# Splitting the experts' weights into fp16 halves on the chip, in place of fp32 matmuls

## The chip, the cores and the metric

The kernel runs on one core of a Trainium2 chip, in one launch. The metric is the device time of an execution in microseconds. Five engines work side by side, each through its own queue in order: TensorE (PE, whose weight loads are shown apart as PEld), VectorE (DVE), ScalarE (ACT), GpSimd (POOL), and SyncE (SP), which only issues the transfers here. They wait for one another through counting semaphores.

## The reference

Two layers of a perceiver: cross-attention to a context of 4096 rows, a self-attention, and a feed-forward part, for 2 batches of 256 latents of width 256, all in fp32. The change concerns the last block, a small attention followed by a mixture of 8 experts:

```python
xf = x.reshape(S, D)                                   # S = 512 rows, D = 256
gates = softmax(xf @ wg); idx = argmax(gates)
loc = ...                                              # place of the row among those of its expert
keep = loc < cap                                       # cap = 64 rows for each expert
disp = zeros((E * cap, D)).at[slot].set(xf, mode='drop').reshape(E, cap, D)
h = einsum('ecd,edf->ecf', disp, w1) + b1[:, None, :]  # D = 256 -> FF = 1024, no activation
y = (einsum('ecf,efd->ecd', h, w2) + b2[:, None, :]).reshape(E * cap, D)
out = where(keep, gate_val * y[slot], 0)
```

Each expert's `w1` is 256 x 1024 and its `w2` 1024 x 256, one MB each, so the 16 matrices make 16 MB.

## The kernel before

Every engine's program is written out by hand, and the order of its instructions is fixed by the source. The low-rank attention (`low_rank_attention`, 16 heads, 2 batches) comes ahead of the last block. It is a software pipeline of 32 steps `i`: PE does scores (L758), turns the normalised probabilities (`turn5`, L770), mixes (`mix5`, L785) and projects (`out5`, L801); ACT takes the exponentials (L1193) and high halves (`hi5` L1200, `oT` L1206); DVE takes maxima (L1644), normalises (`norm5`: L1655, and two `tensor_scalar` of 128x256 at L1657) and makes low halves (`lo5` L1649, `oT_lo` L1705). Its matmuls are already made of fp16 halves: high times high, high times low, low times high. POOL makes the low halves of the heads' weights (`vo_lo`, L1340) in the first 16 steps. In the later steps, tables of step numbers (`LAST_AT`) let in the first pieces of the last block: layer norm, the qkv projection (PE L871, evicted by DVE L1678), and the products of queries and keys, done for one half of the latents by POOL (`queries_times_keys`, L364) and for the other by DVE.

`last_attention` follows. DVE adds the bias to qkv (L1792), multiplies queries with keys (L364), reduces (L1737), applies the softmax in small steps (L1740, L1741, L1746 to L1748), takes the values (L1754, L1756), and applies a layer norm (L1779, L1784). Each of these waits for the one before, and PE fills its time with matmuls whose result nobody reads (`keep_busy`, L470). POOL takes a power for each norm (L1360) and adds biases to rows (L1348, L1349).

`experts`: DVE works out each row's slot and writes a selection matrix `Sm` of zeros and ones (L1827); PE gathers the experts' rows with it (L928), transposed, from the rows' fp16 halves `y1` into PSUM, and ACT and DVE evict that into `disT` in fp32. The experts then go in 4 pairs `g`. `hidden(g)` (L951) multiplies with `w1` in fp32: the first expert of a pair uses the left 64 columns of the array and the second the right 64. ACT and DVE evict (L1261, L1846), `turn_hidden(g)` (L962) turns the result in 8 pieces, DVE adds the bias and evicts (L1853, two of 128x512), and `down(g)` (L976) multiplies with `w2` in fp32, again the pair side by side. `y_out` (DVE L1859, ACT L1237, DVE L1861) and `combine(g)` (L985) bring the rows back. PE's order is hidden 0, turn 0, hidden 1, down 0, turn 1, hidden 2, down 1, combine 0, turn 2, hidden 3, down 2, combine 1, turn 3, down 3, combine 2, combine 3. Two layer norms of DVE and the store end the kernel.

The experts' weights are loaded by SP early enough in whatever part of SBUF has come free: `w1` of experts 4 and 5 before the low-rank attention, 0 to 3 in its middle, `w2` near its end, and `w1` of 6 and 7 once `m_o` has been counted twice.

Of the kernel before, what the change touches and what calls it, by code (L numbers as in the profile page):

```python
# [179 lines left out]

FILL_BETWEEN = {0: 8, 3: 6, 11: 52, 12: 6, 13: 16, 20: 8}
# [24 lines left out]
def build(nc, x, ctx, consts, cols, w_x, w_a, w_ao, b_a, w_f1, w_f2, w_f3, w_f4, w_g1, w_g2, w_g3, w_y, w_yv, b_yv,  # L206
          w_l, w_vo, w_in, w_out, rows6, w_gate, w_e1, b_e1, w_e2, b_e2, consts6, out):
    with ExitStack() as stack:
# [124 lines left out]
        disT = tail[:, 2048:3072].rearrange("p (c n) -> p c n", c=DC)  # L333
        yy = tail[:, 3072:4096].bitcast(F16).rearrange("p (g h n) -> p g h n", g=E6 // 2, h=2)
        hh = [tail[:, 1024:2048], work[:, 3072:4096]]
        hT = [rest[:, 2048 + 1024 * i:3072 + 1024 * i].rearrange("p (f n) -> p f n", f=FC) for i in range(2)]
# [33 lines left out]
        def _(sp):  # L370
# [45 lines left out]
            load_w1 = lambda e: sp.dma_start(w1[:, e], w_e1[e].rearrange("(c p) f -> p c f", p=P)).then_inc(s("w1_in%d" % e), 16)  # L416
            load_w2 = lambda e: sp.dma_start(w2[e], w_e2[e].rearrange("(f p) d -> p f d", p=P)).then_inc(s("w2_in%d" % e), 16)
            def load_vo(q):

                if q >= 2:  # L420
                    sp.wait_ge(s("vo_hi"), 2 * q - 2)
                    sp.wait_ge(s("vo_lo"), 2 * q - 2)
                sp.dma_start(vo_stage[:, 2 * (q % 2):2 * (q % 2) + 2], w_vo[2 * q:2 * q + 2].rearrange("h (c p) n -> p h c n", p=P))\
                    .then_inc(s("x_in%d" % (q % 2)), 16)
# [9 lines left out]
            sp.wait_ge(s("vo_hi"), H5)  # L434
            sp.wait_ge(s("vo_lo"), H5)
# [29 lines left out]
        def _(pe):  # L465
# [259 lines left out]
            def low_rank_attention():  # L725
# [64 lines left out]
                def out5(i):  # L790
                    b = i // H5
                    pe.wait_ge(s("l_ot_lo"), i + 1)
                    pe.wait_ge(s("vo_lo"), min(i + 1, H5))
# [112 lines left out]
            def experts():  # L906
# [17 lines left out]
                for t in range(NT):  # L924
                    pe.wait_ge(s("m_S"), t + 1)
                    for c in range(DC):
                        for h in range(2):
                            mm = pe.matmul(ps[:, c, :], y1[:, h, t, c * P:(c + 1) * P], Sm[:, t, :], start=(t == 0 and h == 0),  # L928
                                           stop=(t == NT - 1 and h == 1))
                        if t == NT - 1:  # L930
                            mm.then_inc(s("m_dis_ps"), 1)
# [6 lines left out]
                def hidden(g):  # L938

                    if g == 0:  # L940
                        pe.wait_ge(s("m_dis"), 2)
# [23 lines left out]
                def down(g):  # L965
# [3 lines left out]
                    for e in pair:  # L969
                        pe.wait_ge(s("w2_in%d" % e), 16 * (1 + (e < SLOTS - 2) * DEEP // SLOTS))  # L970
                    for half in range(2):
                        pe.wait_ge(s("m_hT"), 2 * g + 1 + half)
                        for f in range(half * FC // 2, (half + 1) * FC // 2):
                            for e in pair:
                                o = 64 * (e % 2)
                                mm = pe.matmul(ps[o:o + 64, 4, 0:D], hT[g % 2][:, f, o:o + 64], w2[e][:, f, :],  # L976
                                               start=(f == 0), stop=(f == FC - 1), skip_group_check=True)
# [45 lines left out]
        def _(act):  # L1023
# [143 lines left out]

            def low_rank_attention():
                def vo_hi(h):
# [4 lines left out]
                    act.activation(vo[:, h, 0], vo_stage[:, h % 4], ACT.Copy).then_inc(s("vo_hi"), 1)  # L1174
# [36 lines left out]
                for i in range(2 * H5 + 4):  # L1211
# [22 lines left out]
            def last_part():  # L1234
# [4 lines left out]
                second = leave_pair(1, 7)  # L1239
                next(second)  # L1240
                for j in range(2):
# [3 lines left out]
                    if j == 0:  # L1245
                        next(second)
                    else:
# [4 lines left out]
                act.wait_ge(s("m_dis_ps"), 1)  # L1252
                act.activation(disT[:, 0, :], ps[:, 0, :], ACT.Copy).then_inc(s("m_dis"), 1)
# [3 lines left out]
                for g in range(E6 // 2):  # L1257
# [4 lines left out]
                    if g:  # L1262
                        y_hi(g - 1)
                y_hi(E6 // 2 - 1)
# [23 lines left out]
        def _(pool):  # L1288
# [48 lines left out]
            for h in range(H5):  # L1337

                pool.wait_ge(s("vo_hi"), h + 1)
# [628 lines left out]
```

## Time and profile before

| | us |
|---|---|
| median of 3 timed executions | 567.11 |
| lowest and highest of them | 566.3 and 569.16 |
| the profiled execution's own time | 566.04 |
| its span, first to last instruction | 564.2 |
| granted TensorE clock, mean over the span | 0.985 of full speed |

The span is what all rows of the trace lie in. The profiled execution takes 1.84 us beyond its span, and it is 1.1 us faster than the median of the timed ones. PE is the busiest engine (518.3 us, 92%), then DVE (353.8 us, 63%), ACT (283.5 us, 50%) and POOL (76.7 us, 14%). Part of PE's busy time is the filling matmuls.

### The profile page before, as it was taken

How to read it: one execution, taken by the hardware profiler on the slowest of the kernel's cores; microseconds unless marked ns; L12 is line 12 of the kernel's file. 1: busy time of each engine (PE TensorE's matmuls, PEld its weight loads, DVE VectorE, ACT ScalarE, POOL GpSimd, SP SyncE). 2: the span in 40 equal slices, each digit the busy share in tenths (PEclk: the TensorE clock that was granted, in tenths of full speed). 3: DMA queues.
4: the chain of work that ended last, by engine and by line, in shares of the span. 5: the costliest groups of instructions: out<-in, count | busy, mean ns of one | idle time of the engine just before them, and what ended most of it. 6: DMA issues, size and time to landing. Idle time of an engine off the chain costs nothing.

```text
span 564.2 us, 9402 instructions
## 1 busy us (share of the span) xinstructions
PE 518.3 (92%) x3556; PEld 357.1 (63%) x3556; DVE 353.8 (63%) x848; ACT 283.5 (50%) x616; POOL 76.7 (14%) x66
## 2 busy tenths in 40 slices
PE   7899998998999898999989988899999999888992
PEld 6565664565666554557555776788888778664551
DVE  4874646964449854275555655698878787744335
ACT  3777952537731038494267726788855444011110
POOL 0134131200012000000002400333201011200001
PEclk9999999999999999999999999899999999989997
DMA  8974680000000000000500040222183006950001
GB/s 273 321 198 85 113 187 0 1 2 1 1 1 0 5 25 0 2 1 0 208 17 1 2 150 1 76 75 78 61 316 133 1 1 191 352 204 1 1 0 38
DMA packets 45197, 44.06 MB, mean 78 GB/s; under 512 B 18656, under 2 KB 41184, under 8 KB 45024
## 3 DMA queue, kind: packets, MB, share of 16 engines
q1 hardware_dynamic: 45152, 43.45, 25.3%
q8 instruction: 29, 0.48, 0.4%
q14 instruction: 16, 0.13, 0.1%
HBM read 38.73 MB, written 0.52 MB: 70 GB/s over the span
## 4 chain that ended last, share of the span: by engine, by line
PE 66%; DVE 16%; issue 9%; ACT 6%; POOL 1%; DMA 1%; SPq 0%; DVEq 0%; ACTq 0%; POOLq 0%
PE ps L648 10%; PE ps L677 8%; PE ps L785 7%; PE ps L801 7%; PE ps L662 4%; PE ps L679 4%; PE ps L736 3%; PE ps L770 3%; PE ps L951 3%; PE ps L976 2%; PE ps L758 2%; PE ps L871 1%; DVE mx L1538 1%; ACT arena L1129 1%; ACT arena L1114 1%
## 5 line engine op out<-in xcount | busy, mean ns | idle before, releaser
L648 PE MATMUL ps<-ctx_tr,qtl 128*128 128x512 f16 x384 | 90.7, 379 | 2.1 <-ACT arena L1129 1.4
L1538 DVE TENSOR_REDUCE mx<-arena 128x1 f32<-128x512 f32 x64 | 43.1, 682 | 35.3 <-ACT arena L1129 34.7
L648 PEld LDWEIGHTS ps<-ctx_tr,qtl 128*128 128x128 f16 x384 | 36.7, 98 | 40.8 <-issue 3.2
L1129 ACT ACTIVATE arena<-ps 128x512 f32<-128x512 f32 x64 | 37.9, 596 | 43.9 <-PE ps L648 43.8
L677 PE MATMUL ps<-ctx_nat,pth 128*128 128x512 f16 x172 | 58.4, 379 | 0.0
L1114 ACT ACTIVATE arena<-arena,small 128x512 f32<-128x512 f32 x64 | 45.8, 716 | 6.3 <-DVE small L1547 6.2
L801 PE MATMUL ps<-arena,ctx_tr 128*128 128x256 f16 x384 | 47.2, 273 | 0.1
L679 PE MATMUL ps<-ctx_nat,ptl 128*128 128x256 f16 x172 | 46.9, 273 | 0.0
L662 PE MATMUL ps<-const,arena 128*128 128x128 f32 x256 | 39.1, 275 | 5.8 <-ACT arena L1114 5.1
L1293 POOL TENSOR_TENSOR rstd<-mv,col 128x2 f32<-128x2 f32 x13 | 10.0, 766 | 245.3 <-DVE mv L1398 245.2
L1552 DVE TENSOR_TENSOR ptl<-ps,pth 128x512 f16<-128x512 f32 x43 | 29.5, 688 | 21.6 <-ACT pth L1122 21.4
L662 PEld LDWEIGHTS ps<-const,arena 128*128 128x128 f32 x256 | 29.8, 140 | 17.8 <-ACT arena L1114 10.9
L801 PEld LDWEIGHTS ps<-arena,ctx_tr 128*128 128x128 f16 x384 | 37.5, 98 | 4.6 <-DVE ctx_tr L1705 0.3
L1200 ACT ACTIVATE pth<-ps 128x512 f16<-128x512 f32 x32 | 19.0, 594 | 33.7 <-PE ps L770 33.6
L470 PE MATMUL ps<-ones 128*128 128x256 f16 x244 | 31.7, 291 | 1.1 <-DVE ones L1883 1.1
L1193 ACT ACTIVATE ctx_tr<-ps,small 128x256 f32<-128x256 f32 x64 | 29.6, 471 | 5.7 <-DVE work L1644 5.6
L1122 ACT ACTIVATE pth<-ps 128x512 f16<-128x512 f32 x43 | 25.4, 591 | 9.0 <-PE ps L662 8.8
L470 PEld LDWEIGHTS ps<-ones 128*128 128x128 f16 x244 | 25.2, 104 | 6.2 <-DVE ones L1883 1.1
L677 PE MATMUL ps<-ctx_nat,arena 128*128 128x512 f16 x84 | 28.7, 379 | 0.0
L1644 DVE TENSOR_SCALAR_CACHE_REDUCE work<-ps 128x256 f16<-128x256 f32 x64 | 24.4, 418 | 6.4 <-PE ps L758 6.3
L1552 DVE TENSOR_TENSOR arena<-ps,arena 128x512 f16<-128x512 f32 x21 | 14.5, 690 | 21.0 <-ACT arena L1122 20.8
L677 PEld LDWEIGHTS ps<-ctx_nat,pth 128*128 128x128 f16 x172 | 16.8, 98 | 17.0 <-issue 1.4
(294 smaller groups left out, 1041.0 us busy)
## 6 DMA issues: line engine op xcount, KB each, us to landing
ctx_nat<-in_w_e SPq DMA_DIRECT2D x8, 1024.0 KB, 7.2
ctx_tr<-in_w_e SPq DMA_DIRECT2D x6, 1024.0 KB, 11.8
work<-in_ctx SPq DMA_DIRECT2D x8, 512.0 KB, 5.2
ctx_tr<-in_ctx SPq DMA_DIRECT2D x8, 512.0 KB, 7.4
work<-in_w_vo SPq DMA_DIRECT2D x8, 512.0 KB, 3.8
ctx_nat<-in_w_l SPq DMA_DIRECT2D x4, 512.0 KB, 5.2
arena<-in_w_e SPq DMA_DIRECT2D x2, 1024.0 KB, 7.2
wts<-in_rows SPq DMA_DIRECT2D x1, 1024.0 KB, 14.0
```

The lines of the kernel that those rows point to most:

```text
L470: pe.matmul(ps[:, to, 0:SEQ], o[:, 0:P], o, start=True, stop=True, skip_group_check=True)
L648: mm = pe.matmul(ps[:, n % 2, :], qtl[:, qh, d, u * P:(u + 1) * P], CT[:, t0:t0 + KT, kh, d, :], start=(i == 0 and d == 0), stop=(i == 2 a ...
L662: mm = pe.transpose(ps[:, 4 + j % 2, i * P:(i + 1) * P], S[:, (j) % SRING, i * P:(i + 1) * P], ident)
L677: pe.matmul(ps[:, acc, :], PH[j % PRING][:, i * P:(i + 1) * P], CN[:, t].rearrange("p h d -> p (h d)"), start=(c == 0 and i == 0), stop=Fa ...
L679: mm = pe.matmul(ps[:, acc, 0:D], PL[j % PRING][:, i * P:(i + 1) * P], CN[:, t, 0, :], start=False, stop=(c == NCH - 1 and i == KT - 1), s ...
L785: mm = pe.matmul(ps[:, 4 + i % 2, d * SEQ:(d + 1) * SEQ], xl5[b][:, xh, u, d * P:(d + 1) * P], pt[:, i % 2, pu], start=(n == 0), stop=(n = ...
L801: mm = pe.matmul(ps[:, 6 + b, t * D:(t + 1) * D], oT5[:, i % 2, oh, c, p * P:(p + 1) * P], vo[:, h, vh, c, :], start=(i % H5 == 0 and p == ...
L1114: act.activation(S[:, j % SRING, :], S[:, j % SRING, :], ACT.Exp, bias=ebias[:, u:u + 1], scale=SCALES[L], accum_out=ls[:, u, c:c + 1]).th ...
L1129: act.activation(S[:, n % SRING, :], ps[:, n % 2, :], ACT.Copy).then_inc(s("score_copied"), 1)
L1193: act.activation(P5[:, i % 2, t, :], ps[:, i % 2, t * SEQ:(t + 1) * SEQ], ACT.Exp, bias=nb5[:, i % 2, t:t + 1], scale=1.0 / 16, accum_out= ...
L1538: dve.tensor_reduce(mx[:, u, c:c + 1], S[:, n % SRING, :], AX.X, ALU.max).then_inc(s("score_max"), 1)
L1552: dve.tensor_tensor(PL[j % PRING], ps[:, 4 + j % 2, :], PH[j % PRING], ALU.subtract).then_inc(s("pt_lo"), 1)
```

## The change

The 28 halves of the matrices ("units" of 128x1024 fp32 numbers, half of one expert's `w1` or `w2`) of all experts but `w2` of experts 0 and 1 are split on the chip: ACT writes the fp16 high half (`unit_high`), and POOL subtracts it from the fp32 number and writes the fp16 low half (`unit_low`) over the first half of the unit's own place. The second half of that place becomes the home of a later unit's high half (`HOMES`), so that a later copy of ACT waits for an earlier subtraction of POOL. `disT` and the hidden rows `hT` are kept as fp16 halves too, and each fp32 product becomes three fp16 products.

```diff
+UNITS = [(1, e, k) for e in (4, 5, 0, 1, 2, 3) for k in range(2)] \
+    + [(2, e, k) for e in (6, 7, 2, 3) for k in range(2)] + [(1, e, k) for e in (6, 7) for k in range(2)] \
+    + [(2, e, k) for e in (4, 5) for k in range(2)]
+HOMES = ["a", "b", 0, 1, 2, 3, 4, 5, 6, 7, 8, 9, "c", "d", "e", 10, 11, 12, 13, 14, "f", "g", 15, 16, 17, 18, 19, 20]
+SPLIT_AT = (15, 16, 17, 18, 21, 22, 24, 25, 26, 28, 29, 30)
...
     # PE
-                            mm = pe.matmul(ps[:, c, :], y1[:, h, t, c * P:(c + 1) * P], Sm[:, t, :], start=(t == 0 and h == 0),
-                                           stop=(t == NT - 1 and h == 1))
+                            mm = pe.matmul(ps[:, 6 * h + c, :], y1[:, h, t, c * P:(c + 1) * P], Sm[:, t, :], start=(t == 0),
+                                           stop=(t == NT - 1))
...
                 def hidden(g):
...
-                    for e in pair:
-                        pe.wait_ge(s("w1_in%d" % e), 16)
+                    pe.wait_ge(s("w_lo"), H5 + units_until(1, g))
                     for f in range(2):
                         for c in range(DC):
-                            for e in pair:
-                                o = 64 * (e % 2)
-                                mm = pe.matmul(ps[o:o + 64, f, :], disT[:, c, e * CAP:(e + 1) * CAP],
-                                               w1[:, e, c, f * 512:(f + 1) * 512], start=(c == 0), stop=(c == DC - 1))
+                            for k, (th_, wh) in enumerate(((0, 0), (1, 0), (0, 1))):
+                                for e in pair:
+                                    o = 64 * (e % 2)
+                                    mm = pe.matmul(ps[o:o + 64, f, :], disT[:, th_, c, e * CAP:(e + 1) * CAP],
+                                                   unit_halves(1, e, c)[wh][:, f * 512:(f + 1) * 512],
+                                                   start=(c == 0 and k == 0), stop=(c == DC - 1 and k == 2), skip_group_check=True)
...
     # down(g): g == 0 keeps its fp32 form; for g >= 1 it waits for w_lo and does the same three products with w2
...
     # ACT
+            def unit_high(n):
...
+                act.activation(unit_hi(n), unit_place(n), ACT.Copy).then_inc(s("w_hi"), 1)
...
+                    for n in range(12):
+                        if SPLIT_AT[n] == i:
+                            unit_high(n)
...
+                for n in range(12, 16):
+                    unit_high(n)
...
+                        for f in range(2):
+                            act.wait_ge(s("m_hw"), 2 * g - 1 + f)
+                            act.activation(hT[g % 2][:, 0, 4 * f:4 * f + 4, :], hTw[:, 4 * f:4 * f + 4, :], ACT.Copy).then_inc(s("m_hT_hi"), 1)
...
     # POOL
+            def unit_low(n):
+                pool.wait_ge(s("w_hi"), H5 + n + 1)
+                pool.tensor_tensor(unit_lo(n), unit_place(n), unit_hi(n), ALU.subtract).then_inc(s("w_lo"), 1)
...
                 if k == 0:
                     biases(2, slice(3, 4))
+                    for n in range(12, 17):
+                        unit_low(n)
+                if k == 1:
+                    pool.wait_ge(s("m_S"), NT)
+                    for n in range(17, 28):
+                        unit_low(n)
...
     # DVE
-                    for t in range(2):
-                        o = dve.tensor_scalar(P5[:, i % 2, t, :], P5[:, i % 2, t, :], l5[:, i % 2, t:t + 1], 1024.0, ALU.mult, ALU.mult)
-                    o.then_inc(s("l_norm"), 1)
+                    both = l5[:, i % 2, :].unsqueeze(2).broadcast_to([P, 2, SEQ])
+                    dve.scalar_tensor_tensor(P5[:, i % 2], P5[:, i % 2], 1024.0, both, ALU.mult, ALU.mult).then_inc(s("l_norm"), 1)
...
-                dve.tensor_copy(disT[:, 1, :], ps[:, 1, :]).then_inc(s("m_dis"), 1)
+                for c in range(DC):
+                    dve.wait_ge(s("m_dis_ps"), 2 * c + 2)
+                    dve.tensor_copy(disT[:, 1, c, :], ps[:, 6 + c, :]).then_inc(s("m_dis"), 1)
...
+                    for f in range(2 if g else 0):
+                        dve.wait_ge(s("m_hT_hi"), 2 * g - 1 + f)
+                        dve.tensor_tensor(hT[g % 2][:, 1, 4 * f:4 * f + 4, :], hTw[:, 4 * f:4 * f + 4, :],
+                                          hT[g % 2][:, 0, 4 * f:4 * f + 4, :], ALU.subtract).then_inc(s("m_hT"), 1)
```

ACT's other units stand at these places: 16 to 19 after its second `oT6` eviction (L1230), 20 to 23 after the exponential of the gates (L1251), 24 to 27 after its first eviction of hidden rows. POOL's units 0 to 4 follow the heads' weights, 5 to 8 follow the biases of the first layer norm of the last block, and 9 to 11 those of the second, ahead of its product of queries and keys. The semaphores `vo_hi` and `vo_lo` are now called `w_hi` and `w_lo` and count on; the loads of SP keep their order and their places.

Order on POOL in the changed kernel, from the power of the last block's first residual norm (L1449) to the end of the kernel's splitting; the rows of 128x1024 at L1423 are `unit_low`:

```order
L1449 TENSOR_TENSOR work<-work,col 128x2 [waits m_var]
L1433 TENSOR_TENSOR ctx_tr<-ctx_tr,wts 128x256 [waits xn_turned,w6_in]
L1434 TENSOR_TENSOR X<-X,wts 128x256
L1423 TENSOR_TENSOR arena<-arena,pth 128x1024 [waits w_hi]
L1423 TENSOR_TENSOR arena<-arena,ptl 128x1024 [waits w_hi]
L1423 TENSOR_TENSOR arena<-arena,work 128x1024 [waits w_hi]
L1423 TENSOR_TENSOR arena<-arena,ctx_nat 128x1024 [waits w_hi]
L1423 TENSOR_TENSOR ctx_tr<-ctx_tr,ctx_nat 128x1024 [waits w_hi]
L1449 TENSOR_TENSOR work<-work,col 128x2 [waits m_var]
L1423 TENSOR_TENSOR ctx_tr<-ctx_tr,arena 128x1024 [waits w_hi,m_S]
```

Before, POOL's queue had nothing after the two bias additions (L1433 and L1434 above) but the remaining powers. Now five units stand between them and the next power, and eleven behind that one, of which the list shows the first.

Order on DVE in the experts' part, before, from the eviction of hidden rows of pair 1 to that of pair 2:

```order
L1846 COPY work<-ps 128x512 [waits m_h,m_h_ps]
L1859 TENSOR_TENSOR arena<-ps,wts 128x256 [waits m_y_ps]
L1861 TENSOR_TENSOR ctx_tr<-arena,ctx_tr 128x256 [waits m_y_hi,m_ys]
L1853 TENSOR_TENSOR arena<-ps,wts 128x512 [waits m_hT_ps]
L1853 TENSOR_TENSOR arena<-ps,wts 128x512
L1846 COPY ctx_tr<-ps 128x512 [waits m_hT_ps,m_h,m_h_ps]
```

And in the changed kernel:

```order
L1940 COPY work<-ps 128x512 [waits m_h,m_h_ps]
L1957 TENSOR_TENSOR arena<-ps,wts 128x256 [waits m_y_ps]
L1959 TENSOR_TENSOR ctx_tr<-arena,ctx_tr 128x256 [waits m_y_hi,m_ys]
L1947 TENSOR_TENSOR work<-ps,wts 128x512 [waits m_hT_ps]
L1947 TENSOR_TENSOR work<-ps,wts 128x512
L1952 TENSOR_TENSOR arena<-work,arena 128x512 [waits m_hT_hi] x2
L1940 COPY ctx_tr<-ps 128x512 [waits m_hT_ps,m_h,m_h_ps]
```

Between the bias additions and the next eviction, DVE now has two subtractions whose inputs both lie in SBUF, and they wait for two copies of ACT.

## Rows read from the trace of the kernel before

**Rows 1.** The page's first part: busy us (share) xinstructions of each engine.

```profile
PE 518.3 (92%) x3556; PEld 357.1 (63%) x3556; DVE 353.8 (63%) x848; ACT 283.5 (50%) x616; POOL 76.7 (14%) x66
```

**Rows 2.** Busy by window: us, PE, PEld, DVE, ACT, POOL (xinstructions), PEclk, DMA share, GB/s.

```profile
520.00:540.00 20.00, 19.66 (x136) 10.62 (x138) 7.14 (x13) 2.03 (x4) 0.00 (x0) 1.00 0.00 1
```

**Rows 3.** The chain that ended last, experts' part: start us, us, what.

```profile
486.48 0.88 PE ps L885 x4
...
521.43 3.58 PE ps L951 x16
525.01 3.45 PE ps L976 x32
...
547.30 0.70 DVE arena L1853
...
548.14 3.69 PE ps L976 x32
```

**Rows 4.** The same chain in the low-rank attention: fp16 matmuls of 256 columns.

```profile
451.82 0.76 PE ps L758 x12
...
454.48 1.31 PE ps L801 x12
```

**Rows 5.** Two lines of the context's splitting: duration ns min/median/max, starts us, forms.

```profile
L1102 ACT ACTIVATE ctx_nat<-work x8: 1044/1048/1058, 9.2 to 75.1; 128x1024 f16<-128x1024 f32 x8
L1321 POOL TENSOR_TENSOR ctx_nat<-work,ctx_nat x4: 2129/2131/2136, 53.5 to 76.3; 128x1024 f16<-128x1024 f32 x4
```

**Rows 6.** Timeline of DVE and POOL at 176 us.

```profile
176.42 2.33 DVE L1513 SCALAR_TENSOR_TENSOR wts<-arena,col,wts 128x256 f32<-128x256 f32 x1
176.46 2.01 POOL L1310 TENSOR_TENSOR work<-work 128x1024 f32<-128x1024 f32 x1 [10.45 <-DVE work L1466]
```

**Rows 7.** Line L1513, columns as in rows 5.

```profile
L1513 DVE SCALAR_TENSOR_TENSOR wts<-arena,col,wts x3: 474/483/2331, 148.3 to 176.4; 128x256 f32<-128x256 f32 x3
```

**Rows 8.** Timeline at 316 us: three subtractions of POOL back to back, one addition of DVE.

```profile
316.14 3.57 POOL L1334 TENSOR_TENSOR ctx_nat<-ctx_nat 128x512 f16<-128x512 f32 x3 [5.33 <-ACT ctx_nat L1165]
...
317.57 1.12 DVE L1579 TENSOR_TENSOR X<-X,wts 128x256 f32<-128x256 f32 x1
```

**Rows 9.** Timeline of ACT, DVE and POOL at the end of the low-rank attention.

```profile
463.56 0.60 ACT L1206 ACTIVATE ctx_tr<-ps 128x512 f16<-128x512 f32 x1
...
465.68 0.62 DVE L1657 TENSOR_SCALAR ctx_tr<-ctx_tr,small 128x256 f32<-128x256 f32 x2
...
466.55 0.68 DVE L1649 TENSOR_TENSOR ptl<-ps,pth 128x512 f16<-128x512 f32 x1
466.71 2.36 POOL L364 TENSOR_TENSOR ctx_nat<-ctx_nat 128x1024 f32<-128x1024 f32 x1 [8.72 <-DVE ctx_nat L1678]
...
471.05 0.69 DVE L1649 TENSOR_TENSOR ptl<-ps,pth 128x512 f16<-128x512 f32 x1
```

**Rows 10.** The chain that ended last: the step of PE that needs DVE's L1649.

```profile
472.16 1.32 PE ps L785 x12
```

**Rows 11.** Timeline of POOL, its last bias addition.

```profile
485.77 0.72 POOL L1349 TENSOR_TENSOR X<-X,wts 128x256 f32<-128x256 f32 x1
```

**Rows 12.** Timeline of DVE in the last attention.

```profile
488.44 1.22 DVE L364 TENSOR_TENSOR arena<-ctx_nat 128x1024 f32<-128x1024 f32 x1
489.70 1.22 DVE L1737 TENSOR_REDUCE work<-arena 128x16 f32<-128x1024 f32 x1
490.95 0.17 DVE L1740 TENSOR_TENSOR work<-work 128x8 f32<-128x8 f32 x1
...
491.36 0.88 DVE L1784 SCALAR_TENSOR_TENSOR ctx_tr<-ctx_tr,work,wts 128x256 f32<-128x256 f32 x2
```

**Rows 13.** Busy by window, columns as in rows 2.

```profile
496.00:497.00 1.00, 0.66 (x2) 0.57 (x3) 0.00 (x0) 0.29 (x1) 0.00 (x0) 0.50 1.02 189
```

**Rows 14.** Timeline of PE in the last attention.

```profile
479.51 1.89 PE L851 MATMUL ps<-work,ctx_tr 128*128 128x256 f32 x8
...
496.34 3.40 PE L851 MATMUL ps<-work,ctx_tr 128*128 128x256 f32 x8 [0.69 <-ACT ctx_tr L1230]
```

More of the change, by code:

```diff
@@ L178, in side_steps, with units_until @@
             next(steps[which], None)
+UNITS = [(1, e, k) for e in (4, 5, 0, 1, 2, 3) for k in range(2)] \
[3 more added lines that the diff above has]
+SPLIT_AT = (15, 16, 17, 18, 21, 22, 24, 25, 26, 28, 29, 30)
+WHOLE2 = (0, 1)
+def units_until(layer, pair):
+    return 1 + max(n for n, (l, e, _) in enumerate(UNITS) if l == layer and e // 2 == pair)
 FILL_BETWEEN = {0: 8, 3: 6, 11: 52, 12: 6, 13: 16, 20: 8}
@@ L968, in down @@
                     pair = (2 * g, 2 * g + 1)
-                    for e in pair:
-                        pe.wait_ge(s("w2_in%d" % e), 16 * (1 + (e < SLOTS - 2) * DEEP // SLOTS))
+                    if g == 0:
+                        for e in pair:
+                            pe.wait_ge(s("w2_in%d" % e), 16 * (1 + (e < SLOTS - 2) * DEEP // SLOTS))
+                    else:
+                        pe.wait_ge(s("w_lo"), H5 + units_until(2, g))
                     for half in range(2):
@@ L973, in down @@
                         for f in range(half * FC // 2, (half + 1) * FC // 2):
[L974 to L977, printed above, removed]
+                            if g == 0:
+                                for e in pair:
+                                    o = 64 * (e % 2)
+                                    mm = pe.matmul(ps[o:o + 64, 4, 0:D], hTw[:, f, o:o + 64], w2[e][:, f, :],
+                                                   start=(f == 0), stop=(f == FC - 1), skip_group_check=True)
+                                continue
+                            z = f - half * FC // 2
+                            for k, (th_, wh) in enumerate(((0, 0), (1, 0), (0, 1))):
+                                for e in pair:
+                                    o = 64 * (e % 2)
+                                    mm = pe.matmul(ps[o:o + 64, 4, 0:D], hT[g % 2][:, th_, f, o:o + 64],
+                                                   unit_halves(2, e, half)[wh][:, z * D:(z + 1) * D],
+                                                   start=(f == 0 and k == 0), stop=(f == FC - 1 and k == 2), skip_group_check=True)
                     mm.then_inc(s("m_y_ps"), 1)
@@ L1246, in last_part @@
                         next(second)
+                        for n in range(16, 20):
+                            unit_high(n)
                     else:
@@ L1251, in last_part @@
                 act.activation(e8, e8, ACT.Exp).then_inc(s("m_exp8"), 1)
-                act.wait_ge(s("m_dis_ps"), 1)
-                act.activation(disT[:, 0, :], ps[:, 0, :], ACT.Copy).then_inc(s("m_dis"), 1)
+                for n in range(20, 24):
+                    unit_high(n)
+                for c in range(DC):
+                    act.wait_ge(s("m_dis_ps"), 2 * c + 1)
+                    act.activation(disT[:, 0, c, :], ps[:, c, :], ACT.Copy).then_inc(s("m_dis"), 1)
                 for g in (0, 2):
@@ L1352, in _ @@
             biases(0, slice(0, 2))
+            for n in range(5, 9):
+                unit_low(n)
             layernorm("m", 1)
             biases(1, slice(2, 3))
+            for n in range(9, 12):
+                unit_low(n)
             pool.wait_ge(s("m_qkv0"), 6)
```

67 lines of the change are left out of this document (49 added, 18 removed).

## The prediction

> **What bounds the kernel now.** I read the busy shares first: PE is busy 92% of the span, DVE 63%, ACT 50%, POOL 14% [rows 1]. In the experts' part PE works almost without a gap: 19.66 of 20 us from 520 to 540 [rows 2]. The chain that ended last shows its shape: a `hidden` of 3.58 us, a `down` of 3.45 us, and so on, and only ahead of the last `down` a wait for DVE's eviction [rows 3]. So fewer PE cycles there shorten the kernel, and POOL has the idle time to split weights in. The reader is to see in rows 3 that this part is PE's, and in [rows 12] that the 10 us around 490 are not: there each small step of DVE waits for the one before, PE runs fillers, and anything that holds DVE up is paid in full.
>
> **PE's gain.** An unpaired fp32 matmul of 256 columns costs 0.44 us (L885: two in 0.88), so eight of 512 would take 7.0 us. `hidden` does them in 3.58: the two experts of a pair overlap [rows 3]. An fp16 matmul of 256 columns costs 1.31 / 12 = 0.109 us [rows 4], one of 512 then 0.218. The new `hidden` has 24, in 12 pairs: 12 x 0.218 = 2.6 us if the pairs still overlap. Gain 1.0 us, four times, less a little for the pipeline's end: 3.8 us.
> The new `down` has 48 of 256 columns. Fully overlapped that is 24 x 0.109 = 2.6 us. The nearest fp16 pairs of the trace, the scores that use half the rows each, take 0.76 / 12 = 0.063 us a matmul [rows 4], which gives 3.0 us. I take 3.0, since the number of instructions and weight loads is like theirs: 0.45 us gained for pairs 1 and 2, 0.9 together. Pair 0 keeps fp32.
> For pair 3 nothing covers the new splitting. Before, `down` ended 4.5 us after the turn (551.83 against 547.30) [rows 3]. Now: bias addition 0.70, ACT's copy 0.60, DVE's subtraction 0.70, with the handovers 2.2, then 3.0 and the pipeline's end 0.2: 5.4. A loss of 0.8 (the second halves are ready while the first four pieces are multiplied). For pairs 1 and 2 the next `hidden` of 2.6 us covers these 2.2 us. The `disT` evictions are four of 512 columns in place of two, but side by side on ACT and DVE instead of one after the other: nothing. PE's sum: -3.8 - 0.9 + 0.8 = **-3.9 us**. Bounds: -2.8 (`down` at its old length) to -5.0 (2.6 us each).
>
> **What the splitting costs in itself.** A unit is 1.05 us on ACT and 2.13 us on POOL [rows 5]: 28 of them are 29 and 60 us, on engines with 280 and 487 us idle. ACT's copies fit in the gaps of its steps. The last eleven subtractions run from `m_S` on, 11 x 2.1 = 23 us. `hidden(3)` needs seven of them (15 us) and `down(2)` all; with the lengths above they come an estimated 25 and 27 us after `m_S`. They hold.
>
> **What it costs DVE.** This decides the sign. At 176.42 DVE started an instruction with two inputs in SBUF beside a POOL subtraction-like product of 2.01 us, and it took 2.33 us [rows 6], where the others of that line take 0.48 [rows 7]: it stood until POOL was through. In a train of three POOL instructions, DVE's addition took 1.12 us and ended at 318.69, a microsecond before the train did at 319.71: DVE was let in between two of POOL's [rows 8]. So DVE waits for one instruction at a time, and after each of its own the next of POOL's is in. An instruction with one input in PSUM is not touched: L1649 kept its 0.68 us beside POOL's L364 [rows 9]. The Trainium skill says the same in "SBUF — State Buffer", section "Who interferes with whom": a VectorE instruction with two SBUF inputs contends with a GpSimd instruction that reads SBUF, and the loser blocks for the whole instruction. By that rule, the trace agrees: 2.33 us against 0.48.
>
> Place one, 486 to 496 us. POOL's bias additions end at 486.49 [rows 11], and the copies of units 12 to 15 have been made by then, since ACT idles there. Four subtractions follow: about 486.5, 488.6, 490.7, 492.8, later by what DVE takes between them. DVE's chain is [rows 12]: L364 (two SBUF inputs) at 488.44 slips between or waits; L1737 (one input) runs; L1740 at 490.95 waits for the running subtraction, to 491.6; the next subtraction is in before L1741 is issued, which then waits to 493.7; the fourth is in before L1784, which waits to 495.6 and ends both its instructions at 496.5 against 492.24. That is **+4.3 us**, whichever wins the first race, as the train must pass first. Everything behind (values, projection, norm, slots) follows in series. Unit 16 comes after ACT's eviction and hits nothing. PE idles longer: the granted clock was 0.50 at 496 [rows 13] and L851 took 3.40 us there against 1.89 at 479.5 [rows 14]; with a pause of six us the turning and the logits ahead of it may run at that level too: **+0.5** (0 to 1.7).
>
> Place two, pair 1 of the experts, inside the train of eleven. `y_out`'s L1861 and the two new subtractions have two SBUF inputs. Worked through with steps of 2.1 us, the first waits 0.55, and the first new one 0.5 behind a start already late; `down(1)` starts 1.0 us after `hidden(2)` has ended, and if POOL gets in between the two, its second half is late by as much again: **+1.2** (0 to 3).
>
> Place three, the low-rank attention. `norm5` also reads SBUF twice, before and now. PE turns its result one step later, behind a `mix5` and an `out5` of 1.3 us each [rows 4, 10], and this 2.6 us cover one subtraction of 2.1. Two places do more. Units 5 to 8 stand in a row behind POOL's biases of the first norm: `norm5`, and behind it the qkv eviction L1678, slip by up to 1.9; I take 0.4 of it as uncovered, an estimate from PE's order. Unit 11's copy follows ACT's eviction of 463.56 and ends about 465.2, its subtraction 467.3. `norm5` of 465.68 waits for it, so L1678 is late by 1.5 and POOL's L364 starts at 468.1 instead of 466.71 [rows 9]. DVE's L1737 waits for L364, and L1649 of 471.05 stands behind it in DVE's queue. It ended at 471.74, only 0.4 us before PE's `mix5` of 472.16, and now makes that 1.2 late [rows 9, 10]. Sum **+1.6** (0 to 4). The one instruction of 128x512 for two of 128x256 (0.62 together) costs 0.6 to 0.7: nothing.
>
> **The sum.** -3.9 + 4.3 + 0.5 + 1.2 + 1.6 = +3.7 us, against the profiled execution's 566.04: 569.7. The timed executions had a median of 567.11, but three of the four numbers shown lie between 566.0 and 567.1, so I add to 566.5: **570.2 us**.
>
> **Rivals.**
> *Collisions cost little* (0.23, faster). If DVE is let in first each time and its waits fall into PE's cover, only some 0.7 us remain of 7.6: 566.5 - 3.9 + 0.7 = 563.3. For it: DVE was let in ahead of a queued POOL instruction [rows 8], and most of DVE's instructions have an input in PSUM. Against it: the 2.33 us of [rows 6], and that in [rows 12] four instructions in a row have both in SBUF. Its place is the four subtractions from 486.5. It wins if L1784 ends less than about 1.5 us later than before, counted from the start of L364.
> *Half of them* (0.22, same). The chain at 490 loses one subtraction's length (2.1) or the low-rank part nothing: 566 to 569.5.
> *The fp16 pairs don't overlap* (0.07, much slower). Then `hidden` is 24 x 0.218 = 5.2 us and `down` 48 x 0.109 = 5.2: four times +1.6 and three times +1.8 come to 11.8, with the 7.6 of DVE's waits: 566.5 + 11.8 + 7.6 = 585.9. The rows speak against it: fp16 halves by rows overlap, fp32 halves by columns too [rows 3, 4]. The Trainium skill has a sentence for it: "TensorE: Matmul & The Clock Gate", Part 3, section "The mechanism", says that a weight load overlaps running matmuls only when the row group differs, which that of a column pair doesn't. By that rule no fp32 pair could run at half the price either, and it does.
> *The forecast* (0.48), 567.5 to 574 by its bounds.
>
> **How the numbers follow.** A measurement tells some 0.5% from no change: 564.3 and 569.9. Faster 0.23 is the first rival. Same is the second and the lower part of the forecast's own range: 0.22 + 0.07. Slower is the rest, 0.41 + 0.07. Leaving out the pairs that don't overlap and 5% at each end, the range is 562.5 to 574.
>
> **What would show it.** PE: `hidden` at 2.6 us, `down` of pairs 1 to 3 near 3.0, and a gap of 2 us ahead of `down(3)`. DVE: L1740, L1741 and L1784 of the last attention with durations up to 2 us beside POOL's units; if they keep 0.17 and 0.48, the sum of place one is wrong and the kernel is faster. The new subtractions of pair 1 above their 0.69, those of pairs 2 and 3 at it. POOL: units of 2.1 us, the last done before `down(2)`. `norm5` stretched beside units, and a gap of PE near 472. The prediction fails most easily by the size of place one and by the low-rank part, where the cover is only estimated from the order.

## The result and the profile after

The changed kernel takes 573.12 us (median of 5, 571.19 to 573.65), the kernel before 567.47 in the same comparison (5 runs, 566.3 to 569.68): ratio 1.0088, 95% interval 1.0068 to 1.0108. It is slower. The profiled execution spans 571.3 us against 564.2. The changed kernel's profiled execution is the one at its median; that of the kernel before (566.04) is 1.4 us below its median.

The page's first part, whose rows answer to [rows 1]:

```profile
PE 515.9 (90%) x3636; PEld 360.7 (63%) x3636; DVE 376.4 (66%) x823; ACT 314.0 (55%) x651; POOL 138.9 (24%) x94
```

PE is busy for 2.4 us less, fillers included, and the span is 7.1 us longer: the time went into waits. The timeline of DVE in the last attention of the changed kernel (beside [rows 12]; the two small steps and the two of L1878 took 0.17, 0.17 and 0.88 before):

```profile
490.30 1.22 DVE L402 TENSOR_TENSOR arena<-ctx_nat 128x1024 f32<-128x1024 f32 x1
491.56 1.22 DVE L1831 TENSOR_REDUCE work<-arena 128x16 f32<-128x1024 f32 x1
492.81 0.72 DVE L1834 TENSOR_TENSOR work<-work 128x8 f32<-128x8 f32 x1
493.56 2.05 DVE L1835 TENSOR_TENSOR work<-work 128x16 f32<-128x16 f32 x1
495.65 2.69 DVE L1878 SCALAR_TENSOR_TENSOR ctx_tr<-ctx_tr,work,wts 128x256 f32<-128x256 f32 x2
```

And POOL's at the same place. L1834 and L1835 end when a subtraction does (493.5 and 495.6), and the two of L1878 at 498.34, behind the end of the last at 497.66:

```profile
488.32 2.12 POOL L1423 TENSOR_TENSOR arena<-arena,pth 128x1024 f16<-128x1024 f32 x1
490.41 3.10 POOL L1423 TENSOR_TENSOR arena<-arena,ptl 128x1024 f16<-128x1024 f32 x1
493.47 2.11 POOL L1423 TENSOR_TENSOR arena<-arena,work 128x1024 f16<-128x1024 f32 x1
495.55 2.11 POOL L1423 TENSOR_TENSOR arena<-arena,ctx_nat 128x1024 f16<-128x1024 f32 x1
```

PE's timeline behind it. The bracket is its idle time ahead and what ended that. The turn of four pieces (L870) takes 1.11 us where 0.66 is its time at the full clock (experiments below), and L889 is the line that was L851 in [rows 14]:

```profile
498.39 1.11 PE L870 MATMUL ps<-const,ctx_tr 128*128 128x128 f32 x4 [5.92 <-DVE ctx_tr L1878]
500.20 1.87 PE L935 MATMUL ps<-wts,ctx_tr 128*128 128x8 f32 x8 [0.69 <-ACT ctx_tr L1310]
501.92 1.09 PE L870 MATMUL ps<-const,ctx_tr 128*128 128x128 f32 x4
503.70 3.78 PE L889 MATMUL ps<-work,ctx_tr 128*128 128x256 f32 x8 [0.69 <-ACT ctx_tr L1294]
```

The windows of the changed kernel (columns as in [rows 2]; from 500 to 520 the kernel before was granted 0.91): 0.72 of the clock around the end of the last attention and the routing behind it, and 0.66 in the last `down`.

```profile
500.00:520.00 20.00, 17.45 (x97) 13.12 (x98) 10.06 (x34) 10.17 (x14) 3.44 (x3) 0.72 0.29 105
...
554.00:559.00 5.00, 4.48 (x49) 4.18 (x50) 0.97 (x2) 0.24 (x1) 0.00 (x0) 0.66 0.00 0
```

The chain that ended last, experts' part (beside [rows 3], where `hidden` took 3.58 and `down` 3.45): PE's steps are as short as hoped, `hidden` L989 2.7 and `down` L1026 2.62. But in pair 1 two subtractions of DVE take 3.79, and the last `down` takes 4.49.

```profile
528.49 2.71 PE ps L989 x24
531.20 3.48 PE ps L1019 x32
535.68 0.91 DVE ctx_tr L1959
537.89 3.79 DVE arena L1952 x2
541.72 1.50 PE ps L1026 x24
...
547.78 2.62 PE ps L1026 x48
...
554.52 4.49 PE ps L1026 x48
```

To compare executions I cut each at five points of its timelines: A, the start of the low-rank attention's first exponential; B, the start of DVE's bias addition to qkv in the last attention; C, the end of the pair of L1784 in [rows 12] (now L1878); D, the start of `hidden(0)`; E, the end of the last `combine`. These points have nothing to do with the rivals that are called A to E below. Each length comes from one execution, in us, and is worked out from these starts and ends:

| kernel | A to B | B to C | C to D | D to E | A to E |
|---|---|---|---|---|---|
| before | 141.88 | 4.80 | 22.95 | 39.18 | 208.81 |
| changed | 143.66 | 9.03 | 24.79 | 38.41 | 215.89 |
| small_all | 141.52 | 4.80 | 23.57 | 34.58 | 204.47 |
| small_12_16 | 143.68 | 4.80 | 23.54 | 38.34 | 210.36 |
| small_0_11 | 142.22 | 9.04 | 24.82 | 38.32 | 214.40 |
| small_17_27 | 144.31 | 9.03 | 24.72 | 36.20 | 214.26 |
| filled | 144.46 | 9.05 | 23.56 | 36.82 | 213.89 |
| on_vector | 143.71 | 4.79 | 24.41 | 39.93 | 212.84 |
| on_vector_filled | 143.69 | 4.79 | 23.73 | 38.77 | 210.98 |
| before_one_norm | 141.53 | 4.79 | 23.55 | 39.18 | 209.05 |
| hidden_down1 | 142.95 | 4.80 | 24.71 | 34.88 | 207.34 |
| hidden_down1_filled | 142.95 | 4.79 | 23.01 | 34.89 | 205.64 |
| hidden_only | 142.95 | 4.79 | 24.23 | 35.68 | 207.65 |

The part ahead of A is the same code in all of them, and its length still varies: A lies at 345.4 to 346.3 us in most, but at 347.2 in hidden_only, 347.8 in before_one_norm, 348.9 in hidden_down1_filled, 349.1 in hidden_down1 and 349.3 in on_vector. That is about as much as many of the effects here, so causes are read from the stages and the medians are given beside them.

The stages have the same trouble in small. From 352 to 357 us, just behind A, the kernel before was granted 0.66 of the clock in its execution, and so were small_0_11, small_17_27 and filled; the others were granted all of it. The first line is the kernel before, the second small_all:

```profile
352.00:357.00 5.00, 4.28 (x25) 3.53 (x26) 3.39 (x15) 3.28 (x9) 1.68 (x2) 0.66 0.38 100
```

```profile
352.00:357.00 5.00, 3.71 (x32) 3.18 (x32) 3.42 (x12) 3.77 (x12) 2.27 (x2) 1.00 0.44 105
```

This makes A to B 0.7 to 0.8 longer with no change of the code there: small_17_27 and filled have 144.31 and 144.46 where the changed kernel has 143.66.

### The profile page after: what moved, and what is told of

It is laid out like the page before. It is cut to its first block, busy times and chain, and to the rows that moved or that the text cites. A ratio compares the mean times of both kernels' runs of the same rounds, so it can differ in the third digit from the quotient of the medians.

```text
span 571.3 us, 9620 instructions
## 1 busy us (share of the span) xinstructions
PE 515.9 (90%) x3636; PEld 360.7 (63%) x3636; DVE 376.4 (66%) x823; ACT 314.0 (55%) x651; POOL 138.9 (24%) x94
## 4 chain that ended last, share of the span: by engine, by line
PE 61%; DVE 20%; issue 11%; ACT 6%; POOL 1%; DMA 1%; SPq 0%; DVEq 0%; ACTq 0%; POOLq 0%
PE ps L686 10%; PE ps L715 8%; PE ps L823 6%; PE ps L839 6%; PE ps L700 4%; PE ps L717 4%; PE ps L774 3%; PE ps L808 2%; PE ps L796 2%; PE ps L1026 2%; PE ps L989 1%; DVE mx L1633 1%; DVE ctx_tr L1752 1%; ACT arena L1180 1%; ACT arena L1165 1%
## 5 line engine op out<-in xcount | busy, mean ns | idle before, releaser
L1752 DVE SCALAR_TENSOR_TENSOR ctx_tr<-ctx_tr,small 128x512 f32<-128x512 f32 x32 | 36.0, 1126 | 1.1
L1418 POOL TENSOR_TENSOR arena<-work,arena 128x512 f16<-128x512 f32 x16 | 18.7, 1170 | 53.2 <-ACT arena L1235 53.2
```

Source lines behind the costliest of these rows:

```text
L1752: dve.scalar_tensor_tensor(P5[:, i % 2], P5[:, i % 2], 1024.0, both, ALU.mult, ALU.mult).then_inc(s("l_norm"), 1)
```

## Experiments

My theory: POOL's subtractions hold up those of DVE's instructions that have two operands in SBUF, and the longer waits then cost TensorE its clock. The rivals: ACT's copies or the longer path through three instructions cost it (A); the clock fell for reasons of its own (B); `norm5`'s new form costs it (C).

**The subtractions made small.** In the four kernels, POOL's `unit_low` keeps its place and semaphores and does 8 of 1024 columns, for the units named. PE reads the high half where the low one would be, so it has as many products as before, but these four leave the low halves out of the result: they show where the time goes and can't be used.

```diff
-            return unit_hi(n), unit_lo(n)
+            return unit_hi(n), (unit_hi(n) if 12 <= n < 17 else unit_lo(n))
...
-                pool.tensor_tensor(unit_lo(n), unit_place(n), unit_hi(n), ALU.subtract).then_inc(s("w_lo"), 1)
+                w = 8 if 12 <= n < 17 else 1024    # small_12_16; or n < 12, n >= 17, True
+                pool.tensor_tensor(unit_lo(n)[:, 0:w], unit_place(n)[:, 0:w], unit_hi(n)[:, 0:w], ALU.subtract).then_inc(s("w_lo"), 1)
```

*small_all.* 

> All 28 subtractions of GpSimd on the experts' weights keep their place and their semaphores, but do 8 of 1024 columns each; TensorE reads the high half in place of the low one, so its instructions are as many and as long, and the low halves are left out of the result. Theory 1 (the subtractions hold up VectorE's instructions with two operands in SBUF, and the longer wait then costs TensorE its clock): everything that the change lost comes back, low-rank attention 1.9, units 12 to 15 4.2, the clock behind them 1.8, and in the experts some 2 to 3.5, so 560 to 562 us. Rival A (ScalarE's copies or the longer path through three instructions for the turned hidden states cost it): 570 to 573. Rival B (the clock at half speed in the third down product has causes of its own): about 563 to 564 with that stretch unchanged.

Measured: 563.46 us, ratio to the kernel before 0.994 (0.9913 to 0.9966). That is 1.5 us above the range that I expected; the profiled execution, with 561.51 the fastest of the five, is within it. ACT's copies and the fp16 path are all in it, and it is faster than the kernel before: rival A is out. D to E shows what the fp16 products are worth alone: 34.58 against 39.18, so 4.6 us. The last `down` took 2.8 us at the full clock, which is against rival B as I had put it, although the median is what rival B gave.

*small_12_16.* 

> Only GpSimd's units 12 to 16 (which stand in the last attention) do 8 of 1024 columns, and TensorE reads their high half in place of the low one. Theory 1: the 4.2 us by which VectorE is late between the residual's tensors come back, and the clock's 1.8 with them since TensorE's idle time falls from 5.9 to about 1.7 us: 567 us (566 to 568.5). If the clock is not bound to that wait: 568.9. Rival A (GpSimd's subtractions are no cause): 573.

Measured: 569.53 us, ratio 1.0035 (1.0018 to 1.0052). This is 1 us above the range that I expected; the ten executions lie from 567.79 to 570.55, and the profiled one is at 567.81. From B to C 4.23 us came back, all of it, and from C to D 1.25 of 1.84. DVE's timeline, with the same instructions one line number further down:

```profile
493.01 0.17 DVE L1835 TENSOR_TENSOR work<-work 128x8 f32<-128x8 f32 x1
493.21 0.18 DVE L1836 TENSOR_TENSOR work<-work 128x16 f32<-128x16 f32 x1
493.43 0.88 DVE L1879 SCALAR_TENSOR_TENSOR ctx_tr<-ctx_tr,work,wts 128x256 f32<-128x256 f32 x2
```

*small_0_11.* 

> Only GpSimd's units 0 to 11 (which lie in the low-rank attention) do 8 of 1024 columns, TensorE reads the high half in their place. Theory 1: the low-rank attention ends 1.9 us earlier, the rest stays as it is: 571.2 us. Rival C (that stretch is longer because of the one VectorE instruction that scales both tiles of the scores, 1.13 us in place of twice 0.41): no change, 573.

Measured: 571.86 us, ratio 1.0086 (1.0057 to 1.0115), which by itself tells little. By the stages A to B is 1.44 shorter than in the changed kernel, although this execution has the half-speed stretch behind A and that one has not. Without such a stretch in either, small_all (141.52) and the changed kernel (143.66) differ by 2.14, and that is what units 0 to 11 cost.

It sits in two places. At unit 5 DVE falls back by 0.7 us against small_all and doesn't catch up: `norm5` (L1752) stands there beside POOL's train of three subtractions. The changed kernel's timeline first, then that of small_all:

```profile
438.11 6.76 POOL L1423 TENSOR_TENSOR ctx_nat<-ctx_nat 128x1024 f16<-128x1024 f32 x3
438.24 2.55 DVE L1752 SCALAR_TENSOR_TENSOR ctx_tr<-ctx_tr,small 128x512 f32<-128x512 f32 x1
```

```profile
438.03 0.69 DVE L1753 SCALAR_TENSOR_TENSOR ctx_tr<-ctx_tr,small 128x512 f32<-128x512 f32 x1
```

The other 1.4 us come at unit 11: its subtraction started at 465.55, `norm5` (L1752) at 466.13, and that took 2.10 us. In small_0_11 the same instruction (L1753) takes 0.69. The changed kernel's timeline first, then this one's:

```profile
466.13 2.10 DVE L1752 SCALAR_TENSOR_TENSOR ctx_tr<-ctx_tr,small 128x512 f32<-128x512 f32 x1
```

```profile
465.96 0.69 DVE L1753 SCALAR_TENSOR_TENSOR ctx_tr<-ctx_tr,small 128x512 f32<-128x512 f32 x1
```

*small_17_27.* 

> Only GpSimd's units 17 to 27 (the train beside the experts) do 8 of 1024 columns, TensorE reads the high half in their place. Theory 1: VectorE's pair 1 falls from 3.8 and 0.9 us back to 1.3 and 0.4, 2 us come back (571), and down product 3 stays at half the clock. Rival D (the clock falls there because the stages before it waited for the train): 569 to 569.5 with that product at 2.7 us.

Measured: 571.19 us, ratio 1.0075 (1.0051 to 1.0098). D to E is 2.21 shorter, and DVE's pair 1 is back at its own times:

```profile
536.27 0.43 DVE L1960 TENSOR_TENSOR ctx_tr<-arena,ctx_tr 128x256 f16<-128x256 f32 x1 [0.55 <-ACT ctx_tr L1301]
...
537.99 1.29 DVE L1953 TENSOR_TENSOR arena<-work,arena 128x512 f16<-128x512 f32 x2
```

The last `down` still took 4.4 us, so rival D (the clock falls there because of the train's waits) is out: with the train all but gone the clock was lost all the same.

**The clock.** `FILL[2]` is the number of fillers ahead of the residual's first tiles.

```diff
-FILL = (18, 6, 30, 0, 30)
+FILL = (18, 6, 78, 0, 30)
...
+                    if g == G - 1:
+                        keep_busy(18, 0)
                     down(g)
```

*filled.* 

> The changed kernel with 48 more of TensorE's filler matmuls ahead of the residual's first tiles (78 for 30), and 18 ahead of the third down product, both while TensorE waits for VectorE; they write a bank that nothing reads. Theory 1, its part on the clock: the granted clock stays full from 490 to 512 us, which gives back the 1.8 us behind place one (0.44 on each turn of 128x128, 0.8 on the gate's, 0.35 on the projection), and the third down product takes 2.7 in place of 4.3 us, 1.6 us: 573.1 - 3.4 = 569.7 (568.8 to 571). If the clock has other causes: 573.

Measured: 571.9 us (4 runs, 570.73 to 574.19), ratio 1.009 (1.0062 to 1.0119). The median shows 1.2 of the 3.4 us that I expected and the ratio nothing; the kernel can't be told from the changed one. The stages show 1.23 from C to D and 1.59 from D to E; A to B was 0.8 longer in this execution, with the half-speed stretch behind A. PE's timeline at both places: the turn takes 0.66 again, and the last `down` (48 matmuls) ended at 557.63, 2.80 us after its start.

```profile
490.49 8.68 PE L508 MATMUL ps<-ones 128*128 128x256 f16 x78
499.86 0.66 PE L870 MATMUL ps<-const,ctx_tr 128*128 128x128 f32 x4 [0.69 <-DVE ctx_tr L1880]
...
552.40 2.13 PE L508 MATMUL ps<-ones 128*128 128x256 f16 x18
554.83 0.27 PE L1026 MATMUL ps<-pth,arena 128*64 128x256 f16 x1 [0.30 <-DVE arena L1954]
```

**One part alone.** The kernel before with `norm5` as in the changed one:

```diff
-                    for t in range(2):
-                        o = dve.tensor_scalar(P5[:, i % 2, t, :], P5[:, i % 2, t, :], l5[:, i % 2, t:t + 1], 1024.0, ALU.mult, ALU.mult)
-                    o.then_inc(s("l_norm"), 1)
+                    both = l5[:, i % 2, :].unsqueeze(2).broadcast_to([P, 2, SEQ])
+                    dve.scalar_tensor_tensor(P5[:, i % 2], P5[:, i % 2], 1024.0, both, ALU.mult, ALU.mult).then_inc(s("l_norm"), 1)
```

*before_one_norm.* 

> The kernel before, with one part of the change alone: the scores of both tiles scaled by one VectorE instruction of two operands (1.13 us) in place of two (0.41 each). Theory 1: nothing or 0.3 us, 567.4, since the units' subtractions and not this instruction make the low-rank attention longer. Rival C: 1.5 us or more longer, 569.

Measured: 568.46 us, ratio 1.0016 (1.0 to 1.0032). A to B is 141.53 against 141.88. The two can't be compared as they stand, since the kernel before had its half-speed stretch there and this execution had not. With the stretch in both, small_0_11 (new form, units made small) has 142.22 against 141.88, so the new form costs at most some 0.3 us, not 1.5: rival C is out. The profiled execution's other extra time lies ahead of A (2.2 us) and in 0.6 from C to D, where the granted clock fell elsewhere.

Nor would the old form have spared the waits. In the kernel before its pair of L1657 took 0.62 us alone, and 1.31 beside a low half of the heads' weights (`vo_lo`):

```profile
370.78 0.62 DVE L1657 TENSOR_SCALAR ctx_tr<-ctx_tr,small 128x256 f32<-128x256 f32 x2
373.47 1.16 POOL L1340 TENSOR_TENSOR arena<-work,arena 128x512 f16<-128x512 f32 x1 [3.23 <-ACT arena L1174]
373.73 1.31 DVE L1657 TENSOR_SCALAR ctx_tr<-ctx_tr,small 128x256 f32<-128x256 f32 x2
```

**The subtractions moved to VectorE's own wait.**

```diff
     # DVE
                 values6(1)
+                dve.wait_ge(s("w_lo"), H5 + 12)
+                for n in range(12, 16):
+                    dve.wait_ge(s("w_hi"), H5 + n + 1)
+                    dve.tensor_tensor(unit_lo(n), unit_place(n), unit_hi(n), ALU.subtract).then_inc(s("w_lo"), 1)
                 residual(1, 3)
     # POOL: units 12 to 16 no longer here; 16 to 27 behind m_S, after w_lo has reached H5 + 16
```

*on_vector.* 

> Units 12 to 15 are subtracted by VectorE after it has published the last attention's output (it waits there 4.9 us for TensorE), at some 1.15 us each, and unit 16 moves into GpSimd's train. Theory 1: VectorE's way to the residual's first tiles is undisturbed again (4.2 us), four instructions of 4.6 us fit in the 4.9 us of waiting, and the clock behind gives its 1.8 us: 573.1 - 6.0 + 0 to 1 = 567.6 (566.5 to 569), the same as the kernel before. Rival E (what GpSimd is freed of, VectorE now pays on the path): 570 or more. Theory 1 with a longer train: down product 2 waits up to 2 us, 569.5.

*on_vector_filled.* 

> As the kernel with units 12 to 15 on VectorE, and 12 fillers more ahead of the residual's first tiles, 16 ahead of the third down product. Theory 1: 1.6 us less from the third down product at the full clock and 0 to 1.5 from the half-speed stretch of 3.4 us behind the residual, which the kernel before has as well: 565.5 (564 to 567), faster than the kernel before by 0.3%. If the clock is not bound to TensorE's idle time: as the kernel without these fillers.

Measured: 572.14 us, ratio 1.0079 (1.0051 to 1.0106), and with fillers 568.69, ratio 1.0036 (1.0019 to 1.0054). They missed by 4.5 and 3.2 us, beyond their ranges, and by time on_vector can't be told from the changed kernel. The step itself held: B to C is 4.79, the four instructions took 1.22 us each, and DVE waited another 0.98 us behind them. So rival E's mechanism is out, though the time is what rival E gave. Two things were wrong. The clock behind did not give its 1.8 us: C to D is 24.41, 0.4 shorter than in the changed kernel, although PE's pause had gone back to 1.68 us. And I had taken unit 16 too lightly. At the head of the train it pushed the others by 2.1 us, and `down(1)` waited 2.25 us for DVE where it had waited 0.9; the clock fell within that `down`, which took 4.5 us in place of 3.9. From D to E on_vector is 1.5 us worse than the changed kernel. In on_vector's execution A also lay 3.6 us later than in that one.

**Only the products that pay.** By small_all, `hidden` gains 0.87 us a pair and `down` 0.83 in the pairs that a `hidden` covers, but in the last pair `down` fp32 ends 4.54 us after the turn [rows 3] and fp16 5.07. So the last pair shouldn't be split, and without its four units and those of pair 2 the train is 8 long and over before DVE's pair 1. Unit 11 goes behind POOL's products of queries and keys. The main lines of the edit; the others let ACT and DVE halve the hidden rows of pair 1 alone:

```diff
-    + [(2, e, k) for e in (6, 7, 2, 3) for k in range(2)] + [(1, e, k) for e in (6, 7) for k in range(2)] \
-    + [(2, e, k) for e in (4, 5) for k in range(2)]
+    + [(2, e, k) for e in (2, 3) for k in range(2)] + [(1, e, k) for e in (6, 7) for k in range(2)]
...
     # POOL
             queries_times_keys(pool, 0).then_inc(s("m_prod"), 1)
+            unit_low(11)
...
-                    for n in range(12, 17):
-                        unit_low(n)
                 if k == 1:
                     pool.wait_ge(s("m_S"), NT)
-                    for n in range(17, 28):
+                    for n in range(12, 20):
```

*hidden_down1.* 

> Fp16 halves for the four hidden products and down product 1 alone; the others stay fp32 as before. So 20 units, none of them in the last attention; unit 11 is subtracted after GpSimd's products of queries and keys, the last 8 in the train beside the experts. By theory 1: low-rank attention +0.3 to +0.7 against the kernel before (not 1.8), place one 0, hidden products 4 x 0.87 = -3.5, down product 1 -0.8, the train (16.9 us from 4.3 us ahead of the first hidden product) over before VectorE's pair 1: 0 to +0.5, the clock 0 to +0.6. Sum -3.4: 567.4 - 3.4 = 564.0 us (562.5 to 565.5), faster than both kernels. Rival A (the fp16 path itself costs): 567 or more.

*hidden_down1_filled* (`FILL[2]` 42 for 30). 

> The same with 12 fillers more ahead of the residual's first tiles. If the half-speed stretch of 3.4 us there, which the kernel before has as well, comes of TensorE's 1.7 us of idle time: another 0 to 1.0 us less, 563.4. If not: as without.

*hidden_only.* 

> Fp16 halves for the four hidden products alone, 16 units, 4 of them in the train; every down product fp32. Theory 1: down product 1 takes 3.6 again, but nothing of the train is left beside VectorE's pair 1: 0.8 longer than the one with down product 1, 564.8 us (563.3 to 566.3). If the chain of three instructions for the turned hidden states costs more than down product 1 gains: shorter than that one.

Measured: 565.66, 564.19 and 565.78 us; ratios 0.999 (0.9974 to 1.0005), 0.9957 (0.994 to 0.9975) and 0.9984 (0.9969 to 1.0). The one with fillers is faster than the kernel before, by 0.4%. The first can't be told from the kernel before, where I had expected it faster, and its median is just above the range; the third is within its own. All three are well below the changed kernel's 573.12. D to E is 34.88, 4.3 less than before, as expected; without `down(1)` in fp16 it is 35.68, the expected 0.8 more. A to B is 142.95, 1.1 more than in the kernel before, where I had said 0.3 to 0.7, and 1.4 more than small_all's, which like this one has no half-speed stretch there: 0.7 at unit 5 as in the changed kernel, and 0.7 where unit 11 now stands beside a small step of DVE:

```profile
472.96 2.58 POOL L1417 TENSOR_TENSOR ctx_nat<-ctx_nat 128x1024 f16<-128x1024 f32 x1
474.71 0.85 DVE L1827 TENSOR_TENSOR work<-work 128x8 f32<-128x8 f32 x1
475.60 0.17 DVE L1828 TENSOR_TENSOR work<-work 128x16 f32<-128x16 f32 x1
```

The rest is the clock. PE's timeline of hidden_down1_filled at the residual, then that of hidden_down1: 1.3 us of idle time less, and the same matmuls take 0.66 for 1.11 and 1.99 for 3.78.

```profile
491.60 4.75 PE L508 MATMUL ps<-ones 128*128 128x256 f16 x42
496.72 0.66 PE L870 MATMUL ps<-const,ctx_tr 128*128 128x128 f32 x4 [0.37 <-DVE ctx_tr L1871]
...
499.43 0.66 PE L870 MATMUL ps<-const,ctx_tr 128*128 128x128 f32 x4 [0.30 <-DVE ctx_tr L1843]
500.77 1.99 PE L889 MATMUL ps<-work,ctx_tr 128*128 128x256 f32 x8 [0.69 <-ACT ctx_tr L1294]
```

```profile
496.87 0.66 PE L870 MATMUL ps<-const,ctx_tr 128*128 128x128 f32 x4 [1.68 <-DVE ctx_tr L1871]
...
499.56 1.11 PE L870 MATMUL ps<-const,ctx_tr 128*128 128x128 f32 x4
501.37 3.78 PE L889 MATMUL ps<-work,ctx_tr 128*128 128x256 f32 x8 [0.69 <-ACT ctx_tr L1294]
```

## Why the prediction was right, and where it was off

The direction, the mechanism and the largest term held; the time was 2.9 us low, and what was off are sizes. 573.12 is near the top of the forecast's 567.5 to 574. The measured terms are differences of the table, so they must add up to nearly the 7.1 us between the two profiled spans (7.0 here); the prediction had 3.7. The costs came to 11.6 in place of 7.6, and a gain larger by 0.7 hid a part of that. The two executions also had clocks of their own, which the sum hides.

| term | predicted | measured | from |
|---|---|---|---|
| PE's products | -3.9 | -4.6 | small_all, D to E |
| place one | +4.3 | +4.2 | B to C |
| clock behind it | +0.5 | +1.8 | C to D |
| clock in the last `down` | 0 | +1.6 | filled, D to E |
| place two, the train | +1.2 | +2.2 | small_17_27, D to E |
| place three, low-rank | +1.6 | +1.8 | A to B |

- *PE's gain.* `hidden` took 2.78 from first to last against 3.65, four times 0.87. `down` reached the lower bound of 2.6 rather than 3.0: a column pair costs 0.109 us, so pairs 1 and 2 gained 0.83 each and not 0.45. The last pair lost 0.5, not 0.8. The rival "the fp16 pairs don't overlap" is out: 48 matmuls in 2.62 us is the price of 24. For that rival I had leaned on the Trainium skill ("TensorE: Matmul & The Clock Gate", Part 3, "The mechanism"). Its sentence is about when a weight load overlaps running matmuls; that two matmuls of a column pair couldn't overlap was my reading of it, and the trace is against that.
- *Place one.* Worked out from one row of 2.33 us, and right to 0.1. DVE did wait for one subtraction at a time and POOL's next was in before DVE's next. The rival "collisions cost little" needed the opposite; making these five units small gave 4.2 us back, which shows the cause. The waits up to the ends at 493.5 and 495.6 are also what "SBUF — State Buffer", "Who interferes with whom", says in the Trainium skill: the loser waits for the whole instruction.
- *The clock.* This is the term that was most too small. I saw that PE would idle for six us and priced it at 0.5, with 1.7 as the bound. In fact the granted clock was 0.53 from 497 to 508, over everything behind the pause: turns, logits and projection. The fillers gave 1.2 back, and the other 0.6 also appears in before_one_norm, which splits nothing. How much of the 1.8 comes of the longer pause is not shown, though. With the pause at its old 1.7 us, C to D took 22.95 to 23.57 in four kernels but 24.41, 24.71 and 24.23 in on_vector, hidden_down1 and hidden_only, nearly as much as the changed kernel's 24.79. I did not look at all at what the 2.3 us pause ahead of the last `down` might do, and in this execution it cost 1.6.
- *Place two.* The collisions are where I put them. I let DVE in between two subtractions once; its pair of L1952 took 3.78 for 1.29, so it waited twice, and the `y_out` before it 0.5 more.
- *Place three.* Right in cause, too small in size, and the table's 1.8 hides it. Units 0 to 11 cost 2.1 (the changed kernel against small_all), the new form of `norm5` at most some 0.3, and the half-speed stretch behind A, which only the kernel before had, takes 0.7 off the difference. The 0.4 that I had set aside for units 5 to 8 is 0.7, and the 1.2 for unit 11 is 1.4.

Open: why the last `down` kept its clock in small_all and lost it in small_12_16, small_0_11 and small_17_27, with the same pause of 2.3 us ahead of it in all four. The clock was full there in the two kernels that had fillers in the pause; after small_all, which had none, two cases don't prove that the fillers did it.

## What to carry to other kernels

Work given to an idle GpSimd was free here only where VectorE was not on the path with two-operand instructions in SBUF. List these by place before choosing the order. A wait of VectorE for another engine can take the subtractions instead: on_vector shows it for B to C, though it lost the gain elsewhere. Split only what pays: here 20 units of 28 brought 4.3 of the 4.6 us and met neither of the two costliest places. When a change lengthens a pause of TensorE, what runs behind the pause may run at half the clock, and that has to be in the range of the forecast. Fillers are a cheap trial: PE's next product still waited 0.3 to 0.7 us behind them in the kernels here, so they delayed nothing.

## What the runs showed that I had not expected

Twelve more fillers in a pause of 1.7 us, which was in the kernel before as well, brought 1.7 us from C to D (24.71 to 23.01), and 1.5 by the medians. And the time ahead of A differs by up to 3.9 us between executions of the same code. The granted clock tells them apart. In on_vector (A at 349.3) it was 0.66 from 10 to 15 us and 0.72 from 329 to 335:

```profile
10.00:15.00 5.00, 4.65 (x26) 3.71 (x26) 2.35 (x5) 1.20 (x3) 0.00 (x0) 0.66 1.10 348
329.00:335.00 6.00, 4.56 (x20) 3.12 (x21) 3.27 (x10) 0.00 (x0) 0.35 (x1) 0.72 0.87 307
```

In before_one_norm (A at 347.8) only the second was reduced:

```profile
10.00:15.00 5.00, 4.52 (x35) 3.98 (x36) 4.03 (x6) 2.23 (x3) 0.00 (x0) 1.00 1.10 349
329.00:335.00 6.00, 5.60 (x32) 4.24 (x33) 3.58 (x11) 0.74 (x2) 0.69 (x1) 0.72 0.85 339
```

In small_all (A at 345.4) neither was:

```profile
10.00:15.00 5.00, 4.92 (x39) 4.32 (x38) 3.83 (x5) 2.08 (x2) 0.00 (x0) 1.00 1.10 348
329.00:335.00 6.00, 6.00 (x53) 5.20 (x52) 4.28 (x12) 2.49 (x5) 0.69 (x1) 1.00 0.74 301
```

The two hidden_down1 kernels are like on_vector, hidden_only is like before_one_norm, and the rest like small_all. So a difference of 1 to 2 us between two profiled executions is read by stages, with the granted clock of each stage beside it, or not at all.
